# A transformer block on one core: when the expert weights are split, and in what order the tail runs

## The chip, the core and the metric

The program runs on one core of a Trainium2 chip. The metric is the device time of one execution in microseconds (us), from three runs of the kernel. The engines are TensorE (PE, matrix products; its clock is granted at 1.2 or 2.4 GHz), VectorE (DVE), ScalarE (ACT), GpSimd (POOL) and SyncE (SP), which issues the DMAs. Each engine runs its own list of instructions in order and waits on semaphores that the others count up.

## What is computed

```python
mod = (_silu(L0_c) @ L0_wmod).reshape(L0_c.shape[0], 6, 1, -1)
...
h = _layernorm(x, axis=-1) * (1 + ca) + sa
x = x + ga * _L0_attn_ref(h, L0_attn_Wqkv, L0_attn_bqkv, L0_attn_Wout, L0_attn_bout)
h = _layernorm(x, axis=-1) * (1 + cb) + sb
x = x + gb * _L0_ffn_ref(h, L0_ffn_router_w, L0_ffn_gate_up_proj, ...)
```

x has 4 batches of 512 tokens of width 256. The attention is causal, with 16 heads of 16. The FFN is a mixture: a shared expert that every token passes, and 8 routed experts (gate and up 256 x 1024, down 512 x 256 each), of which each token takes the one with the largest router logit, scaled by its sigmoid. All is float32.

## The kernel before

**Float32 products from f16 halves.** A matrix is scaled by 64 and split in a high f16 half and a low one, the rest; `split_mm` (L1392) forms three products of halves for one float32 product. The weights of the 9 FFN experts (index 8 is the shared one) come as 27 *units* of 1024 columns, 512 KB of float32 each: two for gate and up, one for down per expert. A unit is loaded by SP into one of the slots of `stage`; ScalarE writes its high half to its place in the large tile W (`split_high`, L885); then VectorE (`split_low`, L1153) or GpSimd (L714 scales the staged unit in place, L715 subtracts) writes the low half. The slot is then free for the next load.

**The loops.** Batch by batch (b = -1 to 3), 44 steps each. At step n TensorE computes transposed scores of batch b (`scores_t`, L1490) and plain scores of batch b+1 (`scores`, L1462 and L1464), VectorE takes the maxima of the latter (L1060), ScalarE the exponentials of the former (L838), GpSimd masks them (L693), and TensorE multiplies with the values (L1506). b = -1 has only the plain scores of batch 0, b = 3 only the transposed ones. TensorE has two banks for transposed scores, three in batch 3, so it may be two steps ahead of ScalarE. Side jobs hang on numbered steps (the tables SIDE and LAST): layer norms, the projections of q, k and v, the output projection, the second norm and the router of earlier batches; in batch 3 also the shared expert of batch 0. The halves of q and k and the maxima go through DRAM (`qk_d`, `ng_d`), and so do the rows of the modulation (`mod_d`, `gbb`): SP issues these transfers in one written order. The early tiles of the attention lie in W itself, so a weight unit can only be written to its place when what lies there is no longer needed:

```python
elif n == 6:
    ac.wait_ge(s_pv, 16 * (B - 1))
elif n == 9:
    ac.wait_ge(s_pv, 16 * B)
elif n == 18:
    ac.wait_ge(s_o, NT)
```

Nine units (0 to 8) are therefore split in the loops, three in batch 2 (steps 8, 19, 30) and six in batch 3 (two each at steps 5, 16, 27).

**The tail.** After the loops, parts 4 to 15 of the shared expert's gate and up run (`shared_up`, four 128-column parts per batch; each 12 matmuls of 512 columns), with ScalarE's `silu` (L895) and `hidden_high` (L902) and VectorE's `hidden` (L1168) and `hidden_low` (L1176). Between them stand the last batch's output projection, residual (L1103, L1105), second norm (L1110 to L1127), the transposes of h2 (L1547), router (`logits`, `route`), and the routing itself: `ranks`, `slots` (L1273 to L1282), the one-hots (L1283 to L1292), `inverse` and `places`, which give each of 23 row tiles its tokens. The 18 units 9 to 26 are split here, one or two behind each part. GpSimd gathers the first rows (L763).

**The routed stage.** 23 tiles of 128 gathered rows run through their expert's weights; it starts when all units are split. GpSimd adds the results to the output by indirect DMA (L781).

## Time and profile before

| | us |
|---|---|
| median of three runs | 500.05 (499.14 to 500.27) |
| the profiled execution | 499.79 |
| its span | 498.0 |
| TensorE busy | 405.4 (81%) |
| VectorE busy | 329.5 (66%) |
| ScalarE busy | 227.2 (46%) |
| GpSimd busy | 238.2 (48%) |

Busy time is what the hardware profiler recorded of instructions; a wait is the idle time of an engine ahead of an instruction, put down to what ended last before it. The first exponential starts at 72.02 us, the tail's first matmul at 280.12, the first routed matmul at 371.55.

### The profile page before, as it was taken

The page shows a single profiled execution, that of the slowest core. Times are in us where ns is not written, and L with a number is a line of the kernel's source. Part 1 is how long each engine was busy: PE and PEld are TensorE (multiplying, and loading weights), DVE is VectorE, ACT ScalarE, POOL GpSimd, SP SyncE. Part 2 cuts the span into 40 slices and gives each one's busy share as a digit, 9 for nine tenths or more (in the row PEclk, how much of TensorE's full clock was granted, in tenths as well). Part 3 has the DMA queues.
Part 4 walks back from the last instruction along what each step waited for, and adds up shares of the span by engine and source line. Part 5 has one row for each costly group of instructions (what it writes and reads, how often), then busy time and mean ns, then how long its engine had stood idle before and what let it go on. Part 6 is the DMA issues. An engine that isn't in the chain of part 4 may idle for free.

```text
span 498.0 us, 8328 instructions
## 1 busy us (share of the span) xinstructions
PE 405.4 (81%) x2898; PEld 229.9 (46%) x2898; DVE 329.5 (66%) x622; ACT 227.2 (46%) x403; POOL 238.2 (48%) x273
## 2 busy tenths in 40 slices
PE   3737789899989999889977964855928999999991
PEld 3214335445544455344443431622605666666661
DVE  3779799557968788986676399499383443443441
ACT  2612425776556666557764643273321233233230
POOL 1472843742368543754177368050860356556332
PEclk9978999999999999899999996796869999999998
DMA  7563256847201741132215063224661144443210
GB/s 252 168 161 75 64 111 145 246 134 187 40 0 47 173 78 40 42 120 68 60 47 170 1 205 90 86 84 138 176 194 43 33 80 78 86 78 75 44 21 1
DMA packets 39200, 49.08 MB, mean 99 GB/s; under 512 B 4788, under 2 KB 34100, under 8 KB 39160
## 3 DMA queue, kind: packets, MB, share of 16 engines
q1 hardware_dynamic: 34008, 40.41, 28.6%
q0 software_dynamic: 5152, 8.14, 8.3%
q8 instruction: 25, 0.41, 0.3%
q14 instruction: 15, 0.12, 0.1%
HBM read 33.70 MB, written 15.75 MB: 99 GB/s over the span
## 4 chain that ended last, share of the span: by engine, by line
PE 53%; DVE 19%; POOL 8%; issue 7%; ACT 6%; DMA 5%; SPq 1%; DVEq 0%; POOLq 0%; ACTq 0%
PE bank L1392 31%; PE bank L1506 5%; PE bank L1490 5%; PE bank L1462 4%; DVE W L1153 2%; DVE x_sb L1105 2%; PE bank L1721 2%; DVE mx L1060 2%; POOL W L674 2%; ACT W L813 2%; DVE W L1176 2%; PE bank L1464 2%; DMA qk_d<-W 1%; DVE rowg L1103 1%; DMA stage<-in_wmod 1%
## 5 line engine op out<-in xcount | busy, mean ns | idle before, releaser
L1392 PE MATMUL bank<-W 128*128 128x256 f16 (+2 forms) x756 | 110.0, 300 | 20.8 <-DVE W L1176 10.8
L838 ACT ACTIVATE W<-bank 128x512 f32<-128x512 f32 (+1 forms) x176 | 94.6, 562 | 66.4 <-PE bank L1490 64.6
L1060 DVE TENSOR_REDUCE mx<-bank 128x1 f32<-128x384 f32 (+3 forms) x176 | 104.4, 632 | 24.5 <-PE bank L1464 23.9
L1392 PEld LDWEIGHTS bank<-W 128*128 128x128 f16 x756 | 75.4, 102 | 56.2 <-DVE W L1176 12.0
L693 POOL TENSOR_SCALAR_AFFINE_SELECT W<-W 128x512 f32<-128x512 f32 x64 | 42.7, 670 | 73.8 <-ACT W L838 73.7
L1392 PE MATMUL bank<-W,h2T 128*128 x276 | 68.4, 385 | 10.0 <-DVE h2T L1350 9.2
L1462 PE MATMUL bank<-W 126*128 126x128 f16 (+3 forms) x256 | 64.9, 308 | 12.9 <-DMA W<-qk_d 7.9
L781 POOL DMA_INDIRECT out<-h2T,sidx x23 | 36.4, 1581 | 66.6 <-DVE h2T L1361 66.3
L1490 PE MATMUL bank<-W 128*128 128x512 f16 (+3 forms) x256 | 61.8, 303 | 2.6 <-ACT W L838 2.0
L1392 PE MATMUL bank<-h2T,W 128*128 128x512 f16 x192 | 48.1, 407 | 4.9 <-DVE W L1168 4.9
L1506 PE MATMUL bank<-W 128*32 128x128 f32 (+3 forms) x512 | 47.5, 444 | 4.4 <-POOL W L693 4.3
L1464 PE MATMUL bank<-maskb,identb 128*128 128x128 bf16 (+2 forms) x176 | 43.9, 250 | 0.0
L1392 PEld LDWEIGHTS bank<-W,h2T 128*128 128x128 f16 x276 | 26.7, 98 | 35.9 <-issue 15.4
L1354 DVE TENSOR_TENSOR W<-bank,W 128x512 f16<-128x512 f32 x23 | 15.9, 691 | 37.4 <-ACT W L966 37.4
L966 ACT ACTIVATE W<-bank 128x512 f16<-128x512 f32 x23 | 13.7, 597 | 55.1 <-PE bank L1721 55.1
L1462 PEld LDWEIGHTS bank<-W 126*128 126x128 f16 x256 | 23.6, 100 | 29.9 <-DVE mx L1060 13.0
L1490 PEld LDWEIGHTS bank<-W 128*128 128x128 f16 x256 | 21.4, 98 | 34.2 <-ACT W L838 17.7
L1392 PEld LDWEIGHTS bank<-h2T,W 128*128 128x128 f16 x192 | 19.4, 103 | 29.6 <-issue 6.6
L763 POOL DMA_INDIRECT rowg<-h_d,gidx x23 | 22.8, 991 | 19.0 <-DMA h_d<-rowg 12.5
L827 ACT ACTIVATE W<-bank,bqk 128x512 f16<-128x512 f32 (+1 forms) x32 | 20.3, 684 | 22.4 <-PE bank L1392 20.5
L885 ACT ACTIVATE W<-stage 128x1024 f16<-128x1024 f32 x24 | 24.7, 1055 | 8.4 <-DMA stage<-in_gup 8.3
L1153 DVE SCALAR_TENSOR_TENSOR W<-stage,W 128x1024 f16<-128x1024 f32 x18 | 25.5, 1431 | 3.7 <-ACT W L885 3.5
(166 smaller groups left out, 564.6 us busy)
## 6 DMA issues: line engine op xcount, KB each, us to landing
stage<-in_gup SPq DMA_DIRECT2D x14, 512.0 KB
qk_d<-W SPq DMA_DIRECT2D x48, 128.0 KB
W<-qk_d SPq DMA_DIRECT2D x32, 192.0 KB, 4.3
stage<-in_down SPq DMA_DIRECT2D x7, 512.0 KB
x_sb<-in_x SPq DMA_DIRECT2D x4, 512.0 KB, 9.0
h_d<-gbb SPq DMA_DIRECT2D x4, 512.0 KB, 4.6
h_d<-rowg SPq DMA_DIRECT2D x4, 512.0 KB, 5.7
out<-x_sb SPq DMA_DIRECT2D x4, 512.0 KB, 3.0
```

The source lines that it names most:

```text
L693: g.affine_select(out=d, in_=d, compare_op=ALU.is_ge, fill=0.0, base=0, pattern=[[0, 4], [1, P]], channel_multiplier=-1).then_inc(s_msk, 1)
L763: g.indirect_dma_start(rowg[:, r % RG, :], None, h2_d, bass.IndirectOffsetOnAxis(ap=gidx[:, r:r + 1].bitcast(U32), axis=0)).then_inc(s_gr[ ...
L781: g.indirect_dma_start(out.rearrange("b s n -> (b s) n"), bass.IndirectOffsetOnAxis(ap=sidx[:, r:r + 1].bitcast(U32), axis=0), ry[r % YR], ...
L838: a.activation(PT[j][:, i:i + m, :], t_bank(N)[:, 0:m * w].rearrange("p (i n) -> p i n", i=m), ACT.Exp).then_inc(s_exp, 1)
L885: a.activation(weights(n, 0), staged(n), ACT.Copy, scale=WS).then_inc(s_eh, 1)
L1060: v.tensor_reduce(mx_v[:, b % 2, hp0 // 4, par, i:i + m, t], SB[N % 3][:, 0:m * w].rearrange("p (i n) -> p i n", i=m), AX.X, ALU.max).then ...
L1153: v.scalar_tensor_tensor(weights(n, 1), staged(n), WS, weights(n, 0), ALU.mult, ALU.subtract).then_inc(s_el, 1)
L1392: i = t_.matmul(outp, l, r, start=(n == 0), stop=(n == len(prods) - 1), **kw)
L1462: t_.matmul(bk[:, w * i:w * (i + 1)], qs[r][0:P - 2, hp, par, P * t:w], ks[r][0:P - 2, hp, 0:w], start=(i == 0), stop=False, skip_group_ch ...
L1464: t_.matmul(bk[:, 0:m * w].rearrange("p (i n) -> p i n", i=m)[:, :, w - P:w], identb[:, :], maskb[:, :].unsqueeze(1).to_broadcast([P, m, P ...
L1490: q = t_.matmul(t_bank(N)[:, w * i:w * (i + 1)], ks[r][:, hp, P * j:P * (j + 1)], qs[r][:, hp, par, P * j:S], start=True, stop=True)
L1506: q = t_.matmul(OTb[32 * i:32 * i + 32, P * j:S], v1[b % 2][:, c:c + 32], PT[j][:, i], start=(j == 0), stop=(j == TT - 1), tile_position=( ...
```

## The change

All 27 units are now split in the loops; a table SPLITS gives each its step. They are counted by k, in the order in which they are split: the 18 units 9 to 26 come first (k = 0 to 17, "bounced"), the units 0 to 8 last (k = 18 to 26), the latter straight to their place in W as before. The halves of a bounced unit are written to one of two buffers `ob` in the tile rowg, stored to DRAM (`halves_out`, tensor w_d, 512 KB), and read into their place in W in the tail (`halves_in`), in three groups, as soon as the attention's tiles there are free. `split_high` of unit k waits until the store of k-2 has landed (s_bw). Of 11 bounced units (POOL_LOW) the low half is GpSimd's; ScalarE now also scales their staged unit in a second pass, and GpSimd only subtracts. There are three slots for loads; SP issues store k and then load k+3.

In the tail nothing is split. The last batch's second norm is two fused passes of VectorE (`centre2`, `modulate2`) where GpSimd did half of it; the engines' orders are written out; ScalarE itself issues the store of the last rows of h2; the one-hots are cut off from `slots`.

```diff
-SPLIT_AT = 5
 DEEP = 1
-POOL_UNITS = (9, 11, 13, 15, 17, 19, 21, 23, 25)
+DIRECT = 9
+BOUNCED = 3 * (E + 1) - DIRECT
+POOL_LOW = (0, 1, 2, 4, 6, 9, 10, 12, 14, 15, 17)
...
+SPLITS = {-1: {20: 0, 30: 1, 36: 2},
+          0: {2: 3, 7: 4, 12: 5, 17: 6, 21: 7},
+          1: {2: 8, 7: 9, 12: 10, 17: 11, 21: 12},
+          2: {2: 13, 7: 14, 12: 15, 17: 16, 21: 17, 28: 18, 33: 19, 38: 20},
+          3: {5: 21, 8: 22, 14: 23, 17: 24, 23: 25, 27: 26}}
...
+        w_d = nc.dram_tensor("w_d", [BOUNCED, P, 2, STEP], F16).ap()
...
+        ob = [rowg[:, 2 * k:2 * k + 2, :].rearrange("p r n -> p (r n)").bitcast(F16).rearrange("p (s n) -> p s n", s=2)
+              for k in range(2)]
...
+        def unit(k):
+
+            return k + DIRECT if k < BOUNCED else k - BOUNCED
+
+        def low_done(k):
+
+            by_pool = k in POOL_LOW
+            return (s_elp if by_pool else s_el, sum((m in POOL_LOW) == by_pool for m in range(k + 1)))
...
+        def split_part(k, part):
+
+            if k < BOUNCED:
+                return ob[k % 2][:, part].rearrange("p (s n) -> p s n", s=4)
+            return weights(unit(k), part)
...
-        def early_splits(b, gr):
-
-            if b == B - 2:
-                return range(gr, gr + 1) if gr < 3 else range(0)
-            if b == B - 1:
-                return range(3 + 2 * gr, 5 + 2 * gr) if gr < 3 else range(0)
-            return range(0)
-
-        def ffn_splits(n):
-
-            return (2, 2, 1, 2, 1, 1, 2, 2, 1, 2, 1, 1)[n - FC * DEEP]
...
+            def stage_load(k):
+                e, u = unit_list[unit(k)]
+                if k == 0:
                     sp.wait_ge(s_mp, 1)
-                before = [m for m in range(n) if slot(m) == slot(n)]
-                if before:
-                    sp.wait_ge(*split_done(before[-1]))
-                elif n >= 12:
-                    sp.wait_ge(s_u, FC)
-                dst, s = staged(n), s_eld[slot(n)]
+                if k >= 3:
+                    sp.wait_ge(*low_done(k - 3))
+                dst, s = staged(k), s_eld[k % 3]
...
+            def halves_out(k):
+                sp.wait_ge(*low_done(k))
+                sp.dma_start(w_d[k], ob[k % 2]).then_inc(s_bw[k % 2], 16)
+
+            def halves_in(k):
+                e, u = unit_list[unit(k)]
+                c = place(e)
+                dst = W[:, c:c + WX].rearrange("p (s n) -> p s n", s=2)[:, :, STEP * u:STEP * (u + 1)]
+                sp.dma_start(dst, w_d[k]).then_inc(s_wld, 16)
...
-            loaded = 0
+            for k in range(3):
+                stage_load(k)
...
-                while loaded < {-1: 0, 0: 3, 1: 3, 2: 6, 3: 12}[b]:
-                    expert_load(loaded)
-                    loaded += 1
+                if b == B - 1:
+                    for k in range(BOUNCED + 3, NU):
+                        stage_load(k)
+                elif b >= 0:
+                    for k in range(3 + 5 * b, 8 + 5 * b):
+                        halves_out(k)
+                        stage_load(k + 3)
...
+                    for k in range(3):
+                        halves_out(k)
+                        stage_load(k + 3)
...
-            for n in range(loaded, NU):
-                if n == 14:
-                    rows_out(B - 2)
-                if n == 23:
-                    rows_out(B - 1)
-                expert_load(n)
-
+            for k in range(2):
+                sp.wait_ge(s_bw[k], 8 * BOUNCED)
+            sp.wait_ge(s_pv, 16 * B)
+            for k in range(0, 9):
+                halves_in(k)
+            rows_out(B - 2)
+            sp.wait_ge(s_o, NT)
+            for k in range(9, 12):
+                halves_in(k)
+            sp.wait_ge(s_h2v, TT)
+            for k in range(12, BOUNCED):
+                halves_in(k)
...
-            def split_low(n):
-
-                po.wait_ge(s_eh, n + 1)
-                link(g.tensor_scalar(staged(n), staged(n), WS, 0.0, ALU.mult, ALU.add))
-                g.tensor_tensor(weights(n, 1), staged(n), weights(n, 0), ALU.subtract).then_inc(s_elp, 1)
+            def split_low(k):
+
+                if k not in POOL_LOW:
+                    return
+                po.wait_ge(s_es, sum(m in POOL_LOW for m in range(k + 1)))
+                g.tensor_tensor(split_part(k, 1), staged(k), split_part(k, 0), ALU.subtract).then_inc(s_elp, 1)
...
-            for n in (9, 11):
-                split_low(n)
             rstd(ve2, mv2, rs2, B - 1, s_mv2, s_rstd2)
-            for t in (2, 3):
-                modulate2(B - 1, t)
-            for n in (13, 15, 17, 19):
-                split_low(n)
             def gather(r):
...
+                ac.wait_ge(s_rows3, TT)
+                ac.dma_start(h2_d[S * b:S * (b + 1), 0:H].rearrange("(t p) n -> p t n", p=P), h2s).then_inc(s_h2w, 16)
...
+            def split_high(k):
+                ac.wait_ge(s_eld[k % 3], 32 * (k // 3 + 1))
+                n = unit(k)
+                if 2 <= k < BOUNCED:
+                    ac.wait_ge(s_bw[k % 2], 16 * (k // 2))
...
-                a.activation(weights(n, 0), staged(n), ACT.Copy, scale=WS).then_inc(s_eh, 1)
+                a.activation(split_part(k, 0), staged(k), ACT.Copy, scale=WS).then_inc(s_eh, 1)
+                if k in POOL_LOW:
+                    ac.wait_ge(s_eh, k + 1)
+                    a.activation(staged(k), staged(k), ACT.Copy, scale=WS).then_inc(s_es, 1)
...
+            def centre2(b):
+
+                ve.wait_ge(s_mv2, b + 1)
+                for t in range(TT):
+                    n = TT * b + t
+                    v.scalar_tensor_tensor(h2f[:, t], x_sb[:, n], mv2[:, n, 0:1], bc[:, b % 2, 2 * H:3 * H],
+                                           ALU.subtract, ALU.mult).then_inc(s_hm, 1)
...
+            def modulate2(b):
                 ve.wait_ge(s_hm, TT * (b + 1))
-                link(v.tensor_tensor(h2f[:, t], h2f[:, t], bc[:, b % 2, 2 * H:3 * H], ALU.mult))
-                v.tensor_tensor(h2f[:, t], h2f[:, t], bc[:, b % 2, H:2 * H], ALU.add).then_inc(s_h2v, 1)
+                ve.wait_ge(s_rstd2, b + 1)
+                for t in range(TT):
+                    n = TT * b + t
+                    v.scalar_tensor_tensor(h2f[:, t], h2f[:, t], rs2[:, n:n + 1], bc[:, b % 2, H:2 * H],
+                                           ALU.mult, ALU.add).then_inc(s_h2v, 1)
...
+            hidden(4)
+            attn_low(B - 1, 0)
+            attn_low(B - 1, 1)
+            hidden_low(4)
+            hidden(5)
+            residual(B - 1, 0)
+            residual(B - 1, 1)
+            stats2(B - 1)
+            hidden(6)
+            hidden_low(5)
+            centre2(B - 1)
+            hidden(7)
+            modulate2(B - 1)
+            hidden_low(6)
+            hidden_low(7)
+            hidden(8)
+            h2_low(B - 1, 0)
+            h2_low(B - 1, 1)
+            hidden(9)
+            logits(B - 1)
+            route()
+            shared_out(1, 0)
...
+            shared_up(4)
+            attn_turn(B - 1, 0)
+            attn_turn(B - 1, 1)
+            shared_up(5)
+            output(B - 1, 0)
+            output(B - 1, 1)
+            for n in range(6, 10):
                 shared_up(n)
-                if n == 4:
-                    attn_turn(B - 1, 0)
-                    attn_turn(B - 1, 1)
-                if n == 5:
-                    output(B - 1, 0)
-                    output(B - 1, 1)
-                if n == 8:
-                    shared_down(1, 0)
-                    h2_turn(B - 1, 0)
-                    h2_turn(B - 1, 1)
-                    shared_down(1, 1)
-                    router(B - 1)
-                if n == 9:
-                    ranks()
-                if n == 11:
-                    inverse()
-                if n == 12:
-                    shared_down(2, 0)
-                    shared_down(2, 1)
+            h2_turn(B - 1, 0)
+            h2_turn(B - 1, 1)
+            shared_down(1, 0)
+            router(B - 1)
+            shared_down(1, 1)
+            ranks()
+            for n in range(10, 13):
+                shared_up(n)
+            inverse()
+            shared_up(13)
+            shared_down(2, 0)
+            shared_down(2, 1)
+            shared_up(14)
+            rows_turn(0)
+            shared_up(15)
...
+            pe.wait_ge(*low_done(NU - 1))
+            pe.wait_ge(s_wld, 16 * BOUNCED)
```

**SP's order around batch 0.** From the stacks of batch 1 (W<-qk_d) on. Before:

```order
L479 DMA W<-qk_d 48x4x512 [waits s_qkw1_1]
L479 DMA W<-qk_d 48x4x512 x3
L565 DMA mod_d<-h2T 4x1024 [waits s_m4]
L485 DMA W<-mod_d 128x768 [waits s_md]
L568 DMA gbb<-mod_d 128x4x256
L489 DMA ng_d<-negm 32x2x128 [waits s_neg]
L496 DMA W<-ng_d 2x4x512 [waits s_ngw]
L496 DMA W<-ng_d 2x4x512
L540 DMA h_d<-gbb 128x4x256 [waits s_gbb]
L540 DMA h_d<-gbb 128x4x256 x3
```

Now, with w_d<-rowg the stores of halves and stage<-in_gup, in_down the loads:

```order
L481 DMA W<-qk_d 48x4x512 [waits s_qkw1_1]
L481 DMA W<-qk_d 48x4x512 x3
L520 DMA w_d<-rowg 128x2048 [waits s_elp]
L514 DMA stage<-in_gup 128x1024 [waits s_elp]
L520 DMA w_d<-rowg 128x2048 [waits s_elp]
L514 DMA stage<-in_gup 128x1024 [waits s_elp]
L520 DMA w_d<-rowg 128x2048 [waits s_elp]
L516 DMA stage<-in_down 128x4x256 [waits s_elp]
L579 DMA mod_d<-h2T 4x1024 [waits s_m4]
L487 DMA W<-mod_d 128x768 [waits s_md]
L582 DMA gbb<-mod_d 128x4x256
```

and on from there:

```order
L491 DMA ng_d<-negm 32x2x128 [waits s_neg]
L498 DMA W<-ng_d 2x4x512 [waits s_ngw]
L498 DMA W<-ng_d 2x4x512
L547 DMA h_d<-gbb 128x4x256 [waits s_gbb]
L547 DMA h_d<-gbb 128x4x256 x3
L520 DMA w_d<-rowg 128x2048 [waits s_el]
L514 DMA stage<-in_gup 128x1024 [waits s_el]
```

Three stores and three loads now stand ahead of mod_d, and the fourth store behind the four writes of gbb.

**ScalarE's order at the start of batch 0.** From the last q and k parts of batch 1 on, over the first exponentials (L838 before, L846 now). Before:

```order
L827 ACTIVATE W<-bank,bqk 128x512 [waits s_ql,s_qkw0_1,s_qkv]
L827 ACTIVATE W<-bank,bqk 128x512
L827 ACTIVATE W<-bank,bqk 128x512 [waits s_ql,s_qkv]
L827 ACTIVATE W<-bank,bqk 128x512
L838 ACT_TABLE_LOAD
L838 ACTIVATE W<-bank 128x512 [waits s_st] x4
L838 ACTIVATE W<-bank 128x384 [waits s_st] x4
L838 ACTIVATE W<-bank 128x512 [waits s_st] x3
L838 ACTIVATE W<-bank 128x512 [waits s_pv,s_st]
L838 ACTIVATE W<-bank 128x512 [waits s_st] x3
```

Now (L890 and L893 are the two passes of a split):

```order
L835 ACTIVATE W<-bank,bqk 128x512 [waits s_ql,s_qkv]
L835 ACTIVATE W<-bank,bqk 128x512
L890 ACTIVATE rowg<-stage 128x1024 [waits s_eld1]
L893 ACTIVATE stage<-stage 128x1024 [waits s_eh]
L890 ACTIVATE rowg<-stage 128x1024 [waits s_bw0,s_eld2]
L893 ACTIVATE stage<-stage 128x1024 [waits s_eh]
L846 ACT_TABLE_LOAD
L846 ACTIVATE W<-bank 128x512 [waits s_st] x3
L890 ACTIVATE rowg<-stage 128x1024 [waits s_bw1,s_eld0]
L846 ACTIVATE W<-bank 128x512 [waits s_st]
L846 ACTIVATE W<-bank 128x384 [waits s_st] x4
L890 ACTIVATE rowg<-stage 128x1024 [waits s_bw0,s_eld1]
```

and on from there, to step 14:

```order
L893 ACTIVATE stage<-stage 128x1024 [waits s_eh]
L846 ACTIVATE W<-bank 128x512 [waits s_st] x3
L846 ACTIVATE W<-bank 128x512 [waits s_pv,s_st]
L846 ACTIVATE W<-bank 128x512 [waits s_st]
L890 ACTIVATE rowg<-stage 128x1024 [waits s_bw1,s_eld2]
L846 ACTIVATE W<-bank 128x512 [waits s_st] x2
```

Units 1 and 2 (k) are split ahead of the first exponential, the second of them behind s_bw0, the landing of store 0; units 3, 4 and 5 stand between exponentials, unit 5 behind s_bw1, which then must count store 3.

**VectorE's order in the tail, from the statistics to the transposes of h2.** Before:

```order
L1113 BN_AGGR mv<-st 128x2 [waits s_dv]
L1113 BN_AGGR mv<-st 128x2 x3
L1153 SCALAR_TENSOR_TENSOR W<-stage,W 128x1024 [waits s_eh]
L1168 SCALAR_TENSOR_TENSOR W<-bank,W 128x512 [waits s_hh,s_hl,s_u,s_silu]
L1176 TENSOR_TENSOR W<-W 128x512 [waits s_hid,s_hh]
L1120 TENSOR_SCALAR rowg<-x_sb,mv,rs 128x256 [waits s_rstd2,s_mv2] x4
L1126 TENSOR_TENSOR rowg<-rowg,W 128x256 [waits s_hm]
L1127 TENSOR_TENSOR rowg<-rowg,W 128x256 [waits s_dv]
L1126 TENSOR_TENSOR rowg<-rowg,W 128x256 [waits s_hm]
L1127 TENSOR_TENSOR rowg<-rowg,W 128x256 [waits s_dv]
L1168 SCALAR_TENSOR_TENSOR W<-bank,W 128x512 [waits s_hh,s_hl,s_u,s_silu]
L1176 TENSOR_TENSOR W<-W 128x512 [waits s_hid,s_hh]
```

Now:

```order
L1123 BN_AGGR mv<-st 128x2 [waits s_dv]
L1123 BN_AGGR mv<-st 128x2 x3
L1188 SCALAR_TENSOR_TENSOR W<-bank,W 128x512 [waits s_hh,s_hl,s_u,s_silu]
L1196 TENSOR_TENSOR W<-W 128x512 [waits s_hid,s_hh]
L1138 SCALAR_TENSOR_TENSOR rowg<-x_sb,mv,W 128x256 [waits s_mv2]
L1138 SCALAR_TENSOR_TENSOR rowg<-x_sb,mv,W 128x256 x3
L1188 SCALAR_TENSOR_TENSOR W<-bank,W 128x512 [waits s_hh,s_hl,s_u,s_silu]
L1146 SCALAR_TENSOR_TENSOR rowg<-rowg,rs,W 128x256 [waits s_rstd2,s_hm]
L1146 SCALAR_TENSOR_TENSOR rowg<-rowg,rs,W 128x256 x3
L1196 TENSOR_TENSOR W<-W 128x512 [waits s_hid,s_hh] x2
L1188 SCALAR_TENSOR_TENSOR W<-bank,W 128x512 [waits s_hh,s_hl,s_u,s_silu]
L1151 TENSOR_TENSOR h2T<-bank,h2T 128x512 [waits s_hta] x2
```

The splits (L1153) are gone, the second norm is two passes of four operations for all tiles, and it is followed at once by the operations on which the transposes and the next parts wait.

## Rows read from the trace of the kernel before

**Rows 1.** The page: the span, and the chain that ended last by engine.
```profile
span 498.0 us, 8328 instructions
...
PE 53%; DVE 19%; POOL 8%; issue 7%; ACT 6%; DMA 5%; SPq 1%; DVEq 0%; POOLq 0%; ACTq 0%
```

**Rows 2.** Busy time by stage: stretch, length, engines, then PEclk, DMA share, GB/s.
```profile
122.00:178.00 56.00, 51.19 (x444) 28.40 (x443) 44.37 (x100) 34.70 (x66) 29.88 (x41) 1.00 0.32 74
178.00:229.00 51.00, 47.16 (x403) 25.04 (x402) 41.94 (x88) 30.48 (x57) 25.43 (x37) 0.97 0.21 58
...
280.00:371.50 91.50, 58.19 (x357) 32.83 (x355) 70.56 (x115) 38.53 (x55) 45.88 (x36) 0.80 0.43 130
371.50:498.00 126.50, 114.77 (x736) 74.94 (x736) 49.61 (x99) 33.62 (x68) 51.21 (x38) 0.97 0.29 55
```

**Rows 3.** Timeline of TensorE (PE) in the tail: start, duration, line, operation, idle before.
```profile
280.12 2.75 PE L1392 MATMUL bank<-h2T,W 128*128 128x512 f16 x12
...
298.77 5.15 PE L1392 MATMUL bank<-h2T,W 128*128 128x512 f16 x12 [4.63 <-DVE W L1168]
312.63 5.05 PE L1392 MATMUL bank<-W 128*128 128x256 f16 x24 [8.71 <-DVE W L1176]
...
318.39 2.78 PE L1392 MATMUL bank<-W 128*128 128x256 f16 x24
...
338.03 0.26 PE L1671 MATMUL bank<-ohv,rowg 128*128 128x23 f16 x4 [7.53 <-DVE rowg L1292]
...
359.60 2.75 PE L1392 MATMUL bank<-h2T,W 128*128 128x512 f16 x12
371.55 2.74 PE L1392 MATMUL bank<-W,h2T 128*128 x6 [9.20 <-DVE h2T L1350]
```

**Rows 4.** The lines of the splits: duration in ns, min/median/max, and where.
```profile
L885 ACT ACTIVATE W<-stage x24: 1039/1057/1069, 182.9 to 367.7; 128x1024 f16<-128x1024 f32 x24
...
L1153 DVE SCALAR_TENSOR_TENSOR W<-stage,W x18: 1192/1224/3135, 184.2 to 369.1; 128x1024 f16<-128x1024 f32 x18
...
L714 POOL TENSOR_SCALAR stage<-stage x6: 1045/1054/1479, 285.5 to 361.8; 128x1024 f32<-128x1024 f32 x6
...
L715 POOL TENSOR_TENSOR W<-stage,W x6: 2127/2162/2977, 286.6 to 363.0; 128x1024 f16<-128x1024 f32 x6
```

**Rows 5.** Timeline of VectorE (DVE) in the tail: residual, slots, one-hots.
```profile
293.49 0.41 DVE L1103 SCALAR_TENSOR_TENSOR rowg<-bank,W 128x256 f32<-128x256 f32 x1
...
328.12 0.28 DVE L1273 TENSOR_TENSOR cmpc<-bank,ij 128x128 f32<-128x128 f32 x1
...
337.20 2.49 DVE L1292 TENSOR_TENSOR rowg<-il,poslo 128x512 f16<-128x512 f32 x4
```

**Rows 6.** Timeline of SyncE's DMA issues (SPq) around batch 0.
```profile
76.54 1.77 SPq L479 DMA_DIRECT2D W<-qk_d  x4
78.36 0.34 SPq L565 DMA_DIRECT2D mod_d<-h2T  x1
83.42 0.34 SPq L485 DMA_DIRECT2D W<-mod_d  x1
...
84.28 0.50 SPq L489 DMA_DIRECT2D ng_d<-negm  x1
89.31 0.54 SPq L496 DMA_DIRECT2D W<-ng_d  x2
89.89 3.38 SPq L540 DMA_DIRECT2D h_d<-gbb  x4
```

**Rows 7.** DMA of 70 to 125 us: GB/s in 40 slices of 1.375 us.
```profile
GB/s 16 150 168 172 78 109 203 173 98 0 130 285 219 63 10 287 338 342 344 187 358 396 360 59 12 34 112 139 185 133 18 238 177 170 182 304 227 127 143 188
```

**Rows 8.** Timeline of ScalarE (ACT) around batch 0's start.
```profile
61.99 1.28 ACT L838 ACT_TABLE_LOAD   x1
72.02 2.84 ACT L838 ACTIVATE W<-bank 128x512 f32<-128x512 f32 x5 [8.75 <-PE bank L1490]
...
82.36 1.26 ACT L838 ACTIVATE W<-bank 128x512 f32<-128x512 f32 x2 [0.78 <-PE bank L1490]
```

175 lines of the change are left out of this document (63 added, 112 removed).

## The prediction

> **What bounds the kernel now.** First the page and the table by stage. The profiled execution took 499.79 us, of which its span is 498.0 [rows 1]; the median of the three runs is 500.05, so what I add to the profiled one stands 0.26 below the median, less than a measurement can tell (about 0.2%, 1 us either way, is what it can tell from no change). The chain that ended last is TensorE for 53% and VectorE for 19% [rows 1]. By stage [rows 2]: in the loops (two of the four batches are shown) TensorE is busy 51.2 of 56 and 47.2 of 51 us, so it has 4 to 5 us of slack per batch, VectorE 44.4 and 41.9, ScalarE 34.7 and 30.5. In the tail (280.0 to 371.5, batches 1 to 3 of the shared FFN and the routing) TensorE is busy only 58.2 of 91.5 us at a granted clock of 0.80. In the routed stage it is busy 114.8 of 126.5. The tail holds 33 us of idle TensorE: that is what can be won. The TensorE timeline [rows 3] says who held it: VectorE each time, 4.63 us at 298.77, 8.71 at 312.63, 7.53 at 338.03, 9.20 at 371.55. After such gaps the clock is at its lower level, 1.2 GHz: the twelve matmuls at 298.77 took 5.15 us where those at 280.12 took 2.75, the 24 at 312.63 took 5.05 where those at 318.39 took 2.78.
>
> **The tail: what is removed.** 18 units leave it. On ScalarE each was 1.06 us, on VectorE 9 at 1.22, on GpSimd 9 at 1.05 plus 2.16 [rows 4], all in the same orders as the work that TensorE waits for. Their loads go too, and with them SP's waits for a free stage.
> I build the new tail from TensorE's work. Busy 58.2 us, less the excess of the slow stretches (2.4 and 2.3 by the rows above, and two smaller ones of that kind: about 8 in all), gives 50 us at the upper clock, 2.4 GHz. To this I add the waits that the new order leaves:
> - Up to the transposes of h2 there is none: units 6 to 9 of the first projection (2.6 us each, start to start) cover the residual (0.8 us per tile, from 293.49 on [rows 5]), the statistics and the two fused passes of 4 x 0.42, which end some 18 us after the tail's start.
> - The ranks are issued at about 27.5 us. VectorE then needs a hidden_low that waits for ScalarE's row scaling, slots and one_hots (328.12 to 339.69, 11.6 us together [rows 5]) and three operations of 0.7; TensorE has three units, 7.8 us. It waits 2 us before unit 12 and 4.3 around the inverse, and runs one unit at the lower clock, 2.4 more.
> - At the end unit 15's hidden values, their halves and the first gathered rows: 2.7 us.
> 50 + 2 + 4.3 + 2.4 + 2.7 = 61.4 against 91.5: 30 us less, and the routed stage no longer starts at the lower clock (the six matmuls at 371.55 took 2.74 us, half of it excess [rows 3]), 1 more; I take **30.5 gained**, since each semaphore hop that I rounded away costs a little. Ends: 18 if half of the waits stay, 33 if all idle time goes.
> The read-back is 18 x 512 KB. Writes of that size moved at 287 to 344 GB/s [rows 7]: 9.4 MB in some 30 us, in three groups that start at about 0, 9 and 18 us of the tail, so it has landed by 33 us, and is wanted at 61. Cost nothing; its cover is 28 us. At half the rate it still fits, at a third it would cost some 30. The gathers wait for the last rows of h2, which ScalarE now sends itself and no longer stand behind SP's loads: nothing, the first gather is wanted 20 us later.
>
> **The loops: what is added.** Batch by batch, splits go from 0, 0, 0, 3, 6 to 3, 5, 5, 8, 6 (batch -1 first). Eleven of the 18 also get a second pass on ScalarE, and GpSimd keeps only the subtraction. By durations this is 29 passes of ScalarE, 31 us, seven splits of VectorE, 8.5 us, eleven of GpSimd, 24 us. Most of it has idle time to lie in. The waits are what matters. Each of two buffers must have been stored before the next but one unit is split, and the store is issued by SP in its own order.
> - **Wait A.** Split 2 stands at step 36 of batch -1, ahead of the first exponential in ScalarE's order, and wants store 0. SP issues store 0 only behind the last stacks of batch 1, at 78.36, where the small write of mod_d stands now [rows 6]. That small write had landed by 83.42, behind the same stacks; 512 KB at about 340 GB/s [rows 7] adds 1.5: 84.8. Split 2 and its second pass take 2.1, so the first exponential goes from 72.02 [rows 8] to 86.9, **14.9 us**. ScalarE had only a table load before it, so nothing hides this; TensorE runs two steps ahead and stops. Behind ScalarE stand GpSimd's masks and subtraction 2, and behind that SP's store 2.
> - **Wait B.** Split 5, at step 12 of batch 0, wants store 3. SP issues it behind store 2 (89.3, after subtraction 2 on GpSimd, 2.2), load 5, mod_d and its landing (5 us: 95), the three transfers of 84.28 with their landing (5 us more: 101) and the four writes of gbb to h2_d, 3.38 us to issue and about 7 until they have moved (at 89.89 now). That is 101.2 + 7.1 + 1.5 and the receipt, 1.4: store 3 has landed at 111.2. ScalarE ends exponential 12 at 83.62 now [rows 8]; with wait A, 1.0 for the lower clock less the two steps TensorE had ahead, and 1.5 for splits 3 and 4, at 101.0. So **10.2 us** more.
> - After B again 1.0, and splits 5, 6 and 7 together 2.5. Later stores are issued at least 3 us before they are wanted; I see no third wait.
> - Batches 1 and 2: 8.4 us more of ScalarE each, two more VectorE splits each (2.4), three subtractions on GpSimd each (6.6), one of them at step 21 just ahead of rstd and the low halves of q and k. Not shown before, so bounded: nothing if all of it fits the idle time, 17 if the whole of ScalarE's is on the path. VectorE at 82% is the nearest row [rows 2]: I take its 2.4, one subtraction of 2.2 and 0.4 for double passes, 5 us per batch, **10** together.
> - Batch 3: the same six splits, but one at a time and not two (2 x 1.06 on ScalarE in a row): 2.5 gained, after about 1.2 lost to the first load; **-2.5** as the net, between -6 and +2.
> Sum of the loops: 14.9 + 1.0 + 1.5 + 10.2 + 1.0 + 2.5 + 10 - 2.5 = 38.6. Whole: 38.6 - 30.5 = +8.1, and 499.8 + 8.1 = **508**.
>
> **Two rules weighed.** Store 0 is costed by the small write that landed 5.06 us after its issue [rows 6]. The Trainium skill, "DMA: Bandwidth & Descriptors", section "Anatomy of one DMA — SWDGE (gpsimd) path", fits a DMA from GpSimd's queue at about 2.0 us plus its bytes at 436 GB/s; an estimate from that page is 3.2 us for a store, landed at 81.6, and the whole would be 505. No run here shows such a store.
> When GpSimd's subtraction ran beside it, a VectorE split took up to 3.13 us and not 1.22 [rows 4], 1.9 more. The eight subtractions in batches 0 to 2 could each cost that, 15 us; I charge none beyond the 10 above, because the maxima read one operand, from PSUM. The Trainium skill, "SBUF — State Buffer", speaks of an exclusive shared port pair of VectorE and GpSimd, under which a VectorE operation with two SBUF inputs waits for the whole GpSimd one; by it the sum would go to 523 at most. The row agrees for that pair of operations.
>
> **Rivals.**
> 1. *Only wait A bites* (faster). If ScalarE reaches step 12 as store 3 lands (stores served out of turn, or the gbb writes moving faster than their 7 us), B's 10.2 and its 1.0 go: 508 - 11.2 = 497. For it: the engines moved 396 GB/s at best [rows 7]. Against: SP's order is fixed. The turning point: waits A and B together below 17 us. Chance 0.2 with all that ends below 499.
> 2. *The tail doesn't shrink so far* (slower). VectorE's chained small operations hold TensorE at every unit, or the read-back comes late; 18 won and not 30.5: 520. For it: the chain of slots and one_hots is untouched. Chance 0.13.
> 3. *The cost in the loops eats the gain exactly* (same): no more than 499 to 501, for instance B at 3 us. Chance 0.05.
> 4. *The loops don't take the splits*: more than one wait per batch, since SP is one queue; each costs as B, 10 us: 518. Chance 0.07, within the slower side.
>
> **How the numbers follow.** The forecast, both waits and a tail shorter by about 30, has 0.55, with its own range 502 to 515. Slower than by 0.2%: 0.55 + 0.13 + 0.07 = 0.75; same 0.05; faster 0.2. The range reaches from 494 (A alone, batches 1 and 2 at half price) to 521 (rival 2 with its round-off).
>
> **What would show it.** Right: in ScalarE's waits a DMA w_d<-rowg ahead of split 2 for about 20 us, the first exponential at 85 to 88; a second of 8 to 12 us at step 12; TensorE's idle there, with the lower clock behind each; the tail, from the first unit after the loops to the first routed matmul, in 60 to 64 us at a clock above 0.9; the routed stage unchanged. Wrong: the first exponential near 72, loops that end before 305, or a tail above 70 us.

## The result: 504.0 us against 500.0

| | before | after |
|---|---|---|
| median of five runs each, us | 500.05 (499.14 to 500.35) | 504.01 (503.34 to 504.91) |
| span of the profiled execution | 498.0 | 502.1 |
| first exponential | 72.02 | 87.82 |
| tail's first matmul | 280.12 | 320.40 |
| first routed matmul | 371.55 | 375.36 |

The ratio is 1.0086, with a 95% interval of 1.0067 to 1.0105: slower by some 4 us. Two changes of nearly 40 us stand behind that: the loops end 40.3 us later, the tail is 36.5 us shorter. The routed stage takes 126.7 us, before it took 126.5. (Of the four runs of `f2` below, one took 2173.7 us; it counts in no figure here.)

The page of the profile after, its span, busy time, chain by engine, and the two groups that are new:

```profile
span 502.1 us, 8371 instructions
...
PE 401.1 (80%) x2898; PEld 228.6 (46%) x2898; DVE 314.1 (63%) x620; ACT 236.3 (47%) x414; POOL 230.6 (46%) x262
...
HBM read 43.14 MB, written 25.18 MB: 136 GB/s over the span
...
PE 46%; DVE 14%; POOL 10%; DMA 10%; ACT 9%; issue 7%; SPq 3%; ACTq 0%; DVEq 0%; POOLq 0%
...
L890 ACT ACTIVATE rowg<-stage 128x1024 f16<-128x1024 f32 x18 | 19.0, 1058 | 28.6 <-DMA w_d<-rowg 28.6
...
w_d<-rowg SPq DMA_DIRECT2D x18, 512.0 KB, 3.0
```

DMA has doubled its share of the chain (5% before [rows 1]), and ScalarE's splits were held 28.6 us by the store of w_d alone. Busy time by stage (as in [rows 2]; a batch of the loops, then the tail, then the routed stage):

```profile
152.00:212.00 60.00, 51.26 (x441) 27.94 (x440) 48.43 (x101) 41.58 (x75) 36.79 (x44) 1.00 0.57 157
212.00:268.00 56.00, 47.23 (x398) 24.50 (x395) 46.42 (x91) 36.72 (x65) 32.48 (x40) 0.97 0.39 116
...
320.40:375.30 54.90, 48.67 (x356) 29.93 (x353) 41.79 (x106) 21.60 (x37) 11.49 (x14) 1.00 0.73 250
375.30:502.00 126.70, 114.86 (x736) 75.09 (x736) 49.65 (x99) 33.61 (x68) 51.11 (x38) 0.97 0.28 53
```

TensorE does the same work in batches 1 and 2 (51.3 and 47.2 us busy) and needs 60 and 56 us where it needed 56 and 51. In the tail its clock is 1.00 where it was 0.80, and its idle time has fallen from 33 to 6 us.

**Where the loops lost it.** Timeline of ScalarE (start, duration, line; L890 is the first pass of a split, L893 the second, L846 the exponentials):

```profile
84.36 1.06 ACT L890 ACTIVATE rowg<-stage 128x1024 f16<-128x1024 f32 x1 [20.26 <-DMA w_d<-rowg]
85.45 1.06 ACT L893 ACTIVATE stage<-stage 128x1024 f32<-128x1024 f32 x1
86.52 1.28 ACT L846 ACT_TABLE_LOAD   x1
87.82 1.08 ACT L846 ACTIVATE W<-bank 128x512 f32<-128x512 f32 x2
...
109.97 1.06 ACT L890 ACTIVATE rowg<-stage 128x1024 f16<-128x1024 f32 x1 [8.38 <-DMA w_d<-rowg]
```

and of SyncE's queue, where the stores (L520) stand behind stacks, mod_d and the writes of gbb (L547):

```profile
76.67 1.77 SPq L481 DMA_DIRECT2D W<-qk_d  x4
78.48 0.44 SPq L520 DMA_DIRECT2D w_d<-rowg  x1
...
99.83 3.40 SPq L547 DMA_DIRECT2D h_d<-gbb  x4
103.67 0.91 SPq L520 DMA_DIRECT2D w_d<-rowg  x1
```

Both waits are there, at the forecast places: 20.3 us of idle ScalarE ahead of split 2, which moves the first exponential by 15.8 us, and 8.4 us ahead of split 5. Behind each, TensorE's granted clock is at its lower level (0.50 from 88 to 90 us, and again from 110 to 115). `outs`, ScalarE's copy at the end of each quarter of a batch (L854), marks the positions; of its 16 rows, those at step 4 of batches 1 to 3 and the last one:

```profile
152.05 0.61 ACT L854 ACTIVATE W<-bank 128x512 f32<-128x512 f32 x1
...
211.99 0.61 ACT L854 ACTIVATE W<-bank 128x512 f32<-128x512 f32 x1
...
268.01 0.59 ACT L854 ACTIVATE W<-bank 128x512 f32<-128x512 f32 x1
...
319.26 0.60 ACT L854 ACTIVATE W<-bank 128x512 f32<-128x512 f32 x1 [1.25 <-PE bank L1533]
```

The same four stood at 122.64, 178.06, 229.43 and 278.98 before. So the loss is 29.4 us up to step 4 of batch 1, then 4.5, 4.65 and 1.7 in the three stretches that follow, which are called batches 1, 2 and 3 below.

**Where the tail won it.** TensorE's timeline has three gaps left:

```profile
355.75 0.26 PE L1697 MATMUL bank<-ohv,rowg 128*128 128x23 f16 x4 [0.34 <-DVE rowg L1313]
356.35 2.76 PE L1419 MATMUL bank<-h2T,W 128*128 128x512 f16 x12 [0.34 <-DVE W L1188]
...
375.36 2.74 PE L1419 MATMUL bank<-W,h2T 128*128 x6 [5.61 <-DVE h2T L1377]
```

### The profile page after: what moved, and what is told of

It reads as the page before. It is cut to its first block, busy times and chain, and to the rows that moved or that the text cites. A ratio compares the mean times of both kernels' runs of the same rounds, so it can differ in the third digit from the quotient of the medians.

```text
span 502.1 us, 8371 instructions
## 1 busy us (share of the span) xinstructions
PE 401.1 (80%) x2898; PEld 228.6 (46%) x2898; DVE 314.1 (63%) x620; ACT 236.3 (47%) x414; POOL 230.6 (46%) x262
## 4 chain that ended last, share of the span: by engine, by line
PE 46%; DVE 14%; POOL 10%; DMA 10%; ACT 9%; issue 7%; SPq 3%; ACTq 0%; DVEq 0%; POOLq 0%
PE bank L1419 32%; PE bank L1533 3%; PE bank L1517 2%; DVE mx L1070 2%; DMA w_d<-rowg 2%; DVE x_sb L1115 2%; DMA ng_d<-negm 2%; PE bank L1747 2%; DMA qk_d<-W 2%; ACT W L821 2%; ACT rowg L890 2%; PE bank L1489 2%; POOL W L693 2%; ACT W L846 2%; POOL W L712 2%
## 5 line engine op out<-in xcount | busy, mean ns | idle before, releaser
L846 ACT ACTIVATE W<-bank 128x512 f32<-128x512 f32 (+1 forms) x176 | 93.7, 563 | 51.5 <-PE bank L1517 50.4
L1419 PE MATMUL bank<-W 128*128 128x256 f16 (+2 forms) x756 | 106.1, 293 | 13.8 <-DVE x_sb L1115 5.3
L1419 PEld LDWEIGHTS bank<-W 128*128 128x128 f16 x756 | 73.4, 100 | 46.6 <-issue 13.0
L1517 PE MATMUL bank<-W 128*128 128x512 f16 (+3 forms) x256 | 63.1, 308 | 27.9 <-ACT W L846 27.3
L1489 PE MATMUL bank<-W 126*128 126x128 f16 (+3 forms) x256 | 66.0, 313 | 14.3 <-DMA W<-qk_d 8.2
L712 POOL TENSOR_SCALAR_AFFINE_SELECT W<-W 128x512 f32<-128x512 f32 x64 | 45.9, 722 | 67.0 <-ACT W L846 66.8
L1517 PEld LDWEIGHTS bank<-W 128*128 128x128 f16 x256 | 21.4, 99 | 61.5 <-ACT W L846 42.5
L1419 PE MATMUL bank<-h2T,W 128*128 128x512 f16 x192 | 43.3, 379 | 0.3 <-DVE W L1188 0.3
L735 POOL TENSOR_TENSOR rowg<-stage,rowg 128x1024 f16<-128x1024 f32 x11 | 23.4, 2124 | 24.2 <-ACT stage L893 24.0
L890 ACT ACTIVATE rowg<-stage 128x1024 f16<-128x1024 f32 x18 | 19.0, 1058 | 28.6 <-DMA w_d<-rowg 28.6
## 6 DMA issues: line engine op xcount, KB each, us to landing
qk_d<-W SPq DMA_DIRECT2D x48, 128.0 KB
```

Of the source, the lines that this page charges most:

```text
L712: g.affine_select(out=d, in_=d, compare_op=ALU.is_ge, fill=0.0, base=0, pattern=[[0, 4], [1, P]], channel_multiplier=-1).then_inc(s_msk, 1)
L735: g.tensor_tensor(split_part(k, 1), staged(k), split_part(k, 0), ALU.subtract).then_inc(s_elp, 1)
L846: a.activation(PT[j][:, i:i + m, :], t_bank(N)[:, 0:m * w].rearrange("p (i n) -> p i n", i=m), ACT.Exp).then_inc(s_exp, 1)
L890: a.activation(split_part(k, 0), staged(k), ACT.Copy, scale=WS).then_inc(s_eh, 1)
L1419: i = t_.matmul(outp, l, r, start=(n == 0), stop=(n == len(prods) - 1), **kw)
L1489: t_.matmul(bk[:, w * i:w * (i + 1)], qs[r][0:P - 2, hp, par, P * t:w], ks[r][0:P - 2, hp, 0:w], start=(i == 0), stop=False, skip_group_ch ...
```

## Experiments

Theory: SyncE's one queue, with store k and load k+3 behind unrelated transfers, makes waits A and B; the added work costs the 4.6 us in each of batches 1 and 2; the tail's gain is mostly the split work that left it. Rivals: a wait that is removed only turns up at the next store; the number of buffers is the cause, not the order; the tail's gain is the rewritten order; the read-back has little cover.

The experiments ran in three sets, each on a chip of its own; the kernel before was run in each, at 500.0, 500.1 and 499.7 us. All but one of them build on the change; "new order" is the kernel `e3`. One thing has to be known ahead of them. With the tail of the change, the time from the tail's first matmul to the first routed one goes by the set, whatever was edited:

| set | kernels | tail, us | gap ahead of the first routed matmul |
|---|---|---|---|
| (the result above) | the change | 55.0 | 5.6 |
| first | `e1`, `e2`, `e3` | 55.5 to 55.6 | 6.2 to 6.3 |
| second | `b3`, `b3` with the order, `f1` | 52.0 | 2.6 |
| third | `f2`, `f3`, `q1`, all together | 54.9 | 5.5 to 5.6 |

(The kernel without tail splits, of the first set, and `r1`, of the second, have other tails.) A difference of about 3 us between kernels of the second set and others is therefore not shown to come from the edit. Across sets the end of the loops (the last `outs`) is the better measure, though it too differs by 1.6 us between four traces with nearly the same loops (300.50 to 302.07 in `e3`, `r1`, `f3` and `q1`).

### One wait at a time

Store 0 and load 3 ahead of the first maxima's read-back (`e1`), or store 3 and load 6 ahead of the second's (`e2`):

```diff
                     maxima_out(b + 1, 0)
+                    if b < 0:
+                        halves_out(0)
+                        stage_load(3)
                     maxima(b + 1, 0)
...
-                    for k in range(3):
+                    for k in range(1, 3):
                         halves_out(k)
                         stage_load(k + 3)
```

`e2` does the same with `halves_out(3)` and `stage_load(6)`, between `maxima_out(b, 1)` and `maxima(b, 1)` at b = 0.

> Theory (the place of the stores in SyncE's program makes the waits): with store 0 and load 3 issued right behind the first maxima write (64.5 us) instead of behind the second half of the stacks (78.5), split 2 runs near 70 and the first exponentials come at 73 to 75 instead of 87.8. Store 1 is still issued near 79.5 and lands near 84, so split 3 at step 2 waits 7 to 9 us; wait B shrinks from 8.4 to 2 to 6, since SyncE no longer waits for split 2 before mod_d. Together 9 to 14 us off: 490 to 495 us. Rival 1 (the wait only moves to step 2 and to B, and the loop ends where it ended): 502 to 505 us. Rival 2 (wait A is a whole 15.8 us by itself, nothing behind it): 487 to 489 us.

> Theory: store 3 and load 6 issued between the write and the read-back of the second maxima of batch 0 (near 95 us instead of 103.7) land by 101, so ScalarE's 8.4 us at step 12 fall to under 2; wait A stays at 20.3. 6 to 9 us off: 495 to 498 us. Rival (the later batches had slack that took up wait B, or the maxima's read-back is delayed by as much): 502 to 505 us.

Measured: 500.5 us (1.0005 of before, 0.9984 to 1.0026; 3.5 under the change's 504.0) and 500.7 us (3.3 under). Both gains are far below the 9 to 14 and the 6 to 9 us that were expected, and both times fall between the ranges of theory and rival. ScalarE's splits with a wait, in the first:

```profile
70.99 1.06 ACT L893 ACTIVATE rowg<-stage 128x1024 f16<-128x1024 f32 x1 [6.27 <-DMA w_d<-rowg]
84.61 1.06 ACT L893 ACTIVATE rowg<-stage 128x1024 f16<-128x1024 f32 x1 [8.49 <-DMA w_d<-rowg]
105.50 1.06 ACT L893 ACTIVATE rowg<-stage 128x1024 f16<-128x1024 f32 x1 [7.52 <-DMA w_d<-rowg]
```

and in the second:

```profile
85.04 1.06 ACT L893 ACTIVATE rowg<-stage 128x1024 f16<-128x1024 f32 x1 [20.30 <-DMA w_d<-rowg]
112.49 1.06 ACT L893 ACTIVATE rowg<-stage 128x1024 f16<-128x1024 f32 x1 [3.08 <-DMA w_d<-rowg]
```

In the first, the 20.3 us became 6.3 at split 2 and 8.5 at split 3, which wants store 1, and split 5 still waits 7.5. In the second, the wait left split 5 (step 12), and 3.1 us came back at split 6 (step 17); by the `outs` at step 4 of batch 1 only 3.2 us of the 8.4 are gained. The rival, the wait moves on, holds for most of the price of either one alone.

### The whole order

Stores 0 to 5 with loads 3 to 8, each put where SyncE can issue it soonest: 0 behind the first maxima write, 1 behind its read-back, 2 behind `qk_out(1, 1)`, 3 while mod_d is on its way, 4 and 5 around the second maxima, all ahead of the writes of gbb (`e3`).

```diff
                     maxima(b + 1, 0)
+                if b < 0:
+                    halves_out(1)
+                    stage_load(4)
...
                     sp.dma_start(mod_d[:, :], m4[:, :]).then_inc(s_md, 16)
+                    halves_out(3)
+                    stage_load(6)
                     sp.wait_ge(s_md, 16)
```

> Theory: with stores 0 to 5 each issued as soon as SyncE can after its split, both waits fall to under 4 us together, the first exponentials come near 73 to 75, and the tail's first matmul near 298 instead of 320: 479 to 484 us, which is below both kernels. Rival 1 (the split work in the loops holds them, the waits hide part of it): only 10 to 15 us off, 489 to 494. Rival 2 (earlier stores and loads collide with the stacks and maxima, which come later): gain under 10 us.

Measured: 484.7 us, 0.9685 of before (0.965 to 0.972), 19.3 under the change. The theory's 479 to 484 is just missed, and its "under 4 us together" for the waits by more. The waits for w_d of 0.9 us and more, and the first exponential:

```profile
71.43 1.06 ACT L904 ACTIVATE rowg<-stage 128x1024 f16<-128x1024 f32 x1 [6.37 <-DMA w_d<-rowg]
...
74.89 1.68 ACT L860 ACTIVATE W<-bank 128x512 f32<-128x512 f32 x3
...
90.71 1.06 ACT L904 ACTIVATE rowg<-stage 128x1024 f16<-128x1024 f32 x1 [2.04 <-DMA w_d<-rowg]
98.02 1.06 ACT L904 ACTIVATE rowg<-stage 128x1024 f16<-128x1024 f32 x1 [0.92 <-DMA w_d<-rowg]
```

9.3 us where there were 28.6; the last `outs` is at 301.10, not 319.26. The first of them ends at 71.43, before the exponentials started in the kernel before (72.02), but the two passes and the table load behind it put the first exponential at 74.89. The two single moves gave 3.5 + 3.3; the whole order gives 19.3. Here the queue that serves two buffers had to be moved as a row.

### Buffers instead of order

A third buffer in the unused end of W, so that split k waits for store k-3 (`b3`; every `k % 2` of the buffers becomes `k % 3`), alone and with the new order:

```diff
+        ob.append(early(2 * STEP, F16).rearrange("p (s n) -> p s n", s=2))
...
-                sp.dma_start(w_d[k], ob[k % 2]).then_inc(s_bw[k % 2], 16)
+                sp.dma_start(w_d[k], ob[k % 3]).then_inc(s_bw[k % 3], 16)
```

> The change with a third buffer for the halves and SyncE's order as it was, so that split k waits for store k-3 instead of k-2. Theory (it is the order of SyncE's issues that sets the waits, since load k+3 stands behind store k): split 2 runs near 64 and the first exponentials come near 73, but split 3 at step 2 still waits until load 3 and store 0, issued at 78 to 79, have landed: 84 to 87, a wait of 8 to 12 us, and step 17 may wait for load 6 in place of wait B. 8 to 14 us off: 490 to 496. Rival (the missing buffer is the whole cause): both waits gone, 478 to 483, as in the kernel with the new order.

> Third buffer and the new SyncE order together. Theory: the three waits left in the new order (6.4, 2.0 and 0.9 us) go, unless a load takes their place: 477 to 482 us. Rival (the loads of stage land no earlier, so the waits only change their name): within 1.5 us of the 484.7 of the new order alone.

Measured: 494.2 us alone, 481.2 with the order, each in its theory's range. With the old order the name of the wait changes from the store to the load that stands behind it:

```profile
85.64 1.06 ACT L891 ACTIVATE rowg<-stage 128x1024 f16<-128x1024 f32 x1 [11.85 <-DMA stage<-in_gup]
110.01 1.06 ACT L891 ACTIVATE rowg<-stage 128x1024 f16<-128x1024 f32 x1 [4.36 <-DMA stage<-in_gup]
```

The second row is split 6, at step 17, as foreseen. But both times are of the set with the short tail. By the last `outs` (319.26 in the change) the buffer alone gains 4.8 us (314.50) and the order 18.2 (301.10): of the 9.8 us by the medians, about 3 are the tail. And behind the new order no gain of the third buffer shows in the loops: they end at 302.37, and the 3.5 us between 484.7 and 481.2 are the tail's (55.5 and 52.0). The three waits for w_d are gone, one of 2.2 us for a load has come, and what was won up to there (the third `outs` at 121.02, not 124.06) is lost at TensorE's next wait for the stacks, which SyncE issues at 123.22 here and at 122.47 with two buffers:

```profile
129.60 0.40 PE L1504 MATMUL bank<-W 126*128 126x128 f16 x4 [3.15 <-DMA W<-qk_d]
```

So the number fell in the theory's range by luck. Of the two, the order of SyncE's queue is the cause of most of the loss, and the number of buffers a small part.

### The work that was added to the loops

On the new order, all 18 low halves go to VectorE in one operation (`f1`: `POOL_LOW = ()`, which also removes ScalarE's second pass), or GpSimd scales its 11 units itself (`f2`):

```diff
-                po.wait_ge(s_es, sum(m in POOL_LOW for m in range(k + 1)))
+                po.wait_ge(s_eh, k + 1)
+                link(g.tensor_scalar(staged(k), staged(k), WS, 0.0, ALU.mult, ALU.add))
```

> The new SyncE order, and all 18 low halves on DVE in one operation (1.06 to 1.2 us each) instead of 11 of them on GpSimd behind ScalarE's second pass (1.06 us each). Theory (the 4.6 us that batches 1 and 2 each lost is ScalarE time ahead of the exponentials): 3 passes fewer in each batch, 2 to 3 us less in each, 6 to 9 us off in all: 476 to 479. Rival (DVE holds the loops as much): within 1.5 us of 484.7, or above.

> The new SyncE order, and GpSimd scales the 11 staged units itself (an operation of 1.05 us more for each) instead of ScalarE in a second pass. Theory (ScalarE's time in the loops is what counts): like the kernel with all low halves on DVE, 476 to 480 us, unless GpSimd's pair of operations slows DVE's small operations, then 480 to 484. Rival (GpSimd's masks come late behind the longer pair): 485 to 490.

Measured: 476.8 us (0.9532 of before, 0.9499 to 0.9565) for `f1`, and 484.7 (482.4 to 486.5) for `f2`, just above the second range of its theory and just below its rival's. By the positions of `outs`:

| | step 4 of batch 1 | batch 1 | batch 2 | batch 3 |
|---|---|---|---|---|
| before | 122.6 | 55.4 | 51.4 | 49.6 |
| the change | 152.1 | 59.9 | 56.0 | 51.3 |
| new order | 133.8 | 60.0 | 56.0 | 51.3 |
| and low halves on VectorE | 132.3 | 58.4 | 54.6 | 51.7 |
| or scaled by GpSimd | 136.1 | 58.5 | 54.0 | 52.3 |

Three second passes of ScalarE, 3.2 us, are worth 1.4 to 2.0 us of a batch wherever their work goes, less than the 2 to 3 expected. GpSimd's version gives it back before batch 1: its stores come later, and the waits for them are 12.4 us in all against 9.3. `f1` is 7.9 us faster than the new order by the medians, 10.6 by the two profiled spans; of these only 4.1 lie in the loops, 3.5 in the tail and 2.9 in the routed stage. The tail's part goes by the set, as said above, and the routed stage of that one trace of the new order is the longest of all (128.0 us; 125.1 in `f1`, 125.9 to 127.2 in the others). Within the second set `f1` is 4.4 us below `b3` with the order, so 4 to 5 us is what the edit is shown to give.

About 3 us of each batch's loss stay in `f1` (58.4 and 54.6 us, against 55.4 and 51.4). No run tells apart which of the first passes, VectorE's splits and the transfers holds them. In the trace of the change TensorE waits 3.6 us in batch 1 for the residual, VectorE's L1115, where it waited 0.6 before.

In batch 3 the six splits in near pairs, as before the change (`q1`, one line of SPLITS):

> The new SyncE order, and the six splits of batch 3 in near pairs (steps 5,6,16,17,27,28), as the kernel before had them, instead of steps 5,8,14,17,23,27. Batch 3 took 49.6 us before and 51.3 in the change, with one wait of 1.3 us for a load. Theory (the places of the splits and that wait make the 1.7 us): batch 3 falls to 49.6 to 50.3 us, 1 to 2 us off the 484.7. Rival (it is the units that come in from the batches before, not the places): 51 us or more.

Measured: 486.1 us; batch 3 took 51.8 us (249.25 to 301.02), and 51.2 to 52.7 in the traces of the new order with the places of the change. The rival: it isn't the places. A wait of 1.3 us for the load of unit 21 stayed, since SyncE issues it only behind batch 3's second maxima:

```profile
251.49 1.06 ACT L904 ACTIVATE W<-stage 128x1024 f16<-128x1024 f32 x1 [1.26 <-DMA stage<-in_gup]
```

### The tail: removed work or new order?

The kernel before without the tail's loads and splits, with its order of the tail otherwise kept (one of the cuts in its code):

```diff
-                for _ in range(ffn_splits(n)):
-                    split_high(split)
-                    split += 1
```

> The kernel before, without the loads 12 to 26 and without the 18 splits of the tail (it leaves out the weights of the six experts that they serve: every routed tile takes those of one loaded expert). Order of the tail otherwise as it was. Theory (the tail shrinks because the split work leaves it): tail 56 to 66 us of 91.4, and the DVE operations of slots and one-hots that took 0.8 to 2.0 us beside GpSimd's splits take about 0.2; whole 465 to 475 us. Rival (the rewritten order of the tail gives a good part of the 36.5 us): tail 70 to 80 us, whole 479 to 489.

Measured: 475.1 us. The table by stage, of that tail (280.49 to 347.13):

```profile
280.49:347.13 66.64, 53.68 (x356) 31.12 (x354) 43.26 (x106) 21.48 (x37) 14.20 (x18) 0.92 0.20 64
```

91.4 us becomes 66.6 without the splits, and 55.0 with the rewritten order of the tail as well: 24.8 us of the 36.5 are the removed work, 11.7 the rewritten tail. TensorE still idles 5.1 us for `hidden_low` and 2.5 for the one-hots there, and its clock falls behind them (24 matmuls took 4.46 us and 12 took 5.30, where others of their kind took 2.78 and 2.75). The theory holds for two thirds of the gain, just outside the range that it gave (56 to 66 us), and the rival for one third.

VectorE's chain of small operations, of the kernel before, with GpSimd's splits beside it:

```profile
328.76 0.82 DVE L1276 TENSOR_TENSOR_SCAN ends<-onesE,ntile 128x8 f32<-128x8 f32 x1
329.61 0.17 DVE L1277 TENSOR_TENSOR base<-ends,ntile 128x8 f32<-128x8 f32 x1
329.81 1.98 DVE L1278 TENSOR_SCALAR base<-base 128x8 f32<-128x8 f32 x1
...
334.16 1.98 DVE L1286 TENSOR_TENSOR poslo<-posr,poshi 128x16 f32<-128x16 f32 x1
```

```profile
328.51 1.05 POOL L714 TENSOR_SCALAR stage<-stage 128x1024 f32<-128x1024 f32 x1 [18.22 <-ACT W L885]
329.64 2.13 POOL L715 TENSOR_TENSOR W<-stage,W 128x1024 f16<-128x1024 f32 x1
...
333.97 2.13 POOL L715 TENSOR_TENSOR W<-h2T,W 128x1024 f16<-128x1024 f32 x1
```

and the same operations of the change, where GpSimd is idle:

```profile
348.53 0.17 DVE L1295 TENSOR_TENSOR_SCAN ends<-onesE,ntile 128x8 f32<-128x8 f32 x1
...
348.94 0.17 DVE L1297 TENSOR_SCALAR base<-base 128x8 f32<-128x8 f32 x1
...
351.95 0.18 DVE L1307 TENSOR_TENSOR poslo<-posr,poshi 128x16 f32<-128x16 f32 x1
```

Each long one began while a GpSimd operation ran and ended with it (331.79 and 331.77; 336.14 and 336.10); L1277, which began in the gap of 0.08 us between two of them, took 0.17. The Trainium skill, "SBUF — State Buffer", section "SBUF: two separate sides", states an exclusive lock held for the whole instruction; the traces agree. In the kernel without the splits the same operations take 0.17 to 0.18 as well. With L1284 (0.90 us, 0.18 in the change) the four long ones are 5.0 us longer, which is the whole difference between the 11.6 us of `slots` and one-hots before and the 6.6 of both other kernels.

### The read-back

> The new SyncE order, and each read-back transfer issued three times (the two extra ones go into the idle staging tiles; output unchanged). In the change the 18 read-backs landed some 32 us into the tail and were wanted at 55. Theory (hidden, with 23 us of cover): 36 more at some 400 GB/s are 47 us more, less the cover: 22 to 28 us above the 484.7. Rival (the cover is smaller because gathers and rows share the queue, or the transfers slow other work): over 32 us above; rival 2 (reading costs little more): under 15.

Measured: 515.6 us, 30.9 above, between the theory's 28 and the first rival's 32. In the kernel with the new order alone the traffic (last column, GB/s) ends some 2 us behind 330 (349 GB/s from 331 to 332, 67 from 332 to 333):

```profile
325.00:330.00 5.00, 5.00 (x82) 4.16 (x79) 3.97 (x13) 3.43 (x7) 0.00 (x0) 1.00 1.00 367
330.00:335.00 5.00, 5.00 (x25) 2.25 (x23) 4.55 (x16) 2.62 (x5) 0.00 (x0) 1.00 0.45 164
335.00:340.00 5.00, 4.32 (x34) 2.23 (x33) 5.00 (x12) 1.53 (x3) 0.00 (x0) 1.00 0.02 5
```

Its first routed matmul is at 357.78: 26 us of cover. With three times the reads that matmul is released at 387.67, so the last transfer that it needs ended some 56 us later; less the cover, 30. In the change itself the traffic falls off shortly behind 350 (385 GB/s up to there, 121 from 350 to 351), 30 us into the tail, so the read-back is hidden there too, with a cover of about 25 us where 28 were forecast. One thing was not expected: the rows of batch 2 stand behind nine read-backs in SyncE's queue, and ScalarE, which must wait for them, stood 18.1 us there, TensorE 17.2. In the change that place costs nothing only because the nine go out in 8 us.

### The last gap, and all together

> The new SyncE order, and TensorE transposes the first gathered rows behind the last shared unit instead of ahead of it. The idle time ahead of the first routed matmul is 5.6 to 6.3 us in four traces and 2.6 in four others. Theory (the first gather lands late in some of them, and the transposes hold the last shared unit behind them): the gap is 2.6 to 4 us here, 0 to 3 us off the 484.7. Rival (it is something else, or the rows now come too late): gap 5.5 us or more, 484 to 487.

> New SyncE order, third buffer, all low halves on DVE, and the first gathered rows transposed behind the last shared unit. If the four gains add (19.3, 3.5, 7.9 and 0 to 3 us from 504.0): 470 to 474 us. Rival (the third buffer and the DVE halves take the same time away): 474 to 477.

`f3` (`rows_turn(0)` behind `shared_up(15)`): 486.1 us, gap 5.6, as the 5.5 of the three others of its set. Not the place of the transposes. All together: 481.1 us (five runs, 480.9 to 482.8), above both ranges and above the 476.8 of `f1`, though its loops end 0.9 us earlier (last `outs` at 296.05 and 296.97). The sum that was expected had counted the second set's shorter tail, 3.5 us, as a gain twice. Against the 486.1 of `f3` and `q1`, in its own set, it is 5.0 us faster. Its tail has the long gap and `f1`'s the short one; the first routed matmuls of `f1`, then of all together:

```profile
350.10 1.47 PE L1433 MATMUL bank<-W,h2T 128*128 x6 [2.64 <-DVE h2T L1391]
```

```profile
352.08 2.74 PE L1434 MATMUL bank<-W,h2T 128*128 x6 [5.53 <-DVE h2T L1392]
```

The gap was 2.6 us in four traces (`b3`, `b3` with the order, `f1`, and the kernel without tail splits) and 5.5 to 6.3 in eight. Where it is long, `silu` and `hidden` of the last two shared units wait some 3 us each for TensorE, though its records show no pause. TensorE's records are the same on both sides: its last shared unit starts 46.60 us into the tail in `b3`, `e3`, `q1` and the change. With the tail of the change the gap was the same in all kernels of one set and different between the sets; the kernel without tail splits, with the older order of the tail, had 2.6 in the first set. What decides it stays open, and so does whether it is the chip: no kernel with this tail was run in two sets.

## Why the prediction came out as it did

Forecast 508, measured 504.0, in the range and on the forecast side. The two waits, the longer loops and the shorter tail are all there, at their places. That the total is off by 4 only is partly luck: the tail came out 6.0 us shorter than forecast, and the loops 1.7 and the routed stage 0.3 longer, against it. Three smaller steps failed: the sign of batch 3, the 1 us counted for the routed stage, and what was to hold batches 1 and 2.

| term | forecast | measured |
|---|---|---|
| wait A (first exponential) | 14.9 | 15.8 |
| wait B | 10.2 | 8.4 |
| the loops up to batch 1, with both | 31.1 | 29.4 |
| batches 1 and 2 | +10 | +9.2 |
| batch 3 | -2.5 | +1.7 |
| loops | +38.6 | +40.3 |
| tail (the forecast with 1 us of the routed stage) | -30.5 | -36.5 |
| routed stage | in the tail's | +0.3 |

- **Wait A.** Store 0 landed at 84.36 (forecast 84.8). What was missed is the 1.28 us table load, which stood ahead of the wait in the kernel before [rows 8] and stands behind split 2 now: "ScalarE had only a table load before it" is the sentence that should have charged it.
- **Wait B** came at step 12 of batch 0 and was 8.4 us: ScalarE was there at 101.6 (forecast 101.0), and store 3 had landed by 109.97 (111.2). From the start of the gbb writes to the landing it took 10.1 us, as summed (7.1 + 1.5 + 1.4), though no row gave the 1.4 of the receipt. What was put 1.4 us too late is that start, 101.2 and not 99.83: store 2 was issued at 88.73 (89.3), and mod_d had landed by 93.80 (95).
- **Batches 1 and 2.** The size held, the parts didn't. Moving eleven more low halves to VectorE made the loops shorter, which speaks against the 2.4 us for its splits, and the second passes of ScalarE, put at 0.4, are 1.4 to 2.0 us of each batch. The other 3 us of each are not explained by a run.
- **Batch 3** is a step that failed. The 2.5 us forecast as gained were 1.7 lost, within the bounds of -6 to +2: one split at a time instead of two gained nothing, and near pairs gave no other length. A wait of 1.3 us for the load of unit 21 stands in that batch, where no split of the kernel before waited; no run took it away, so its part in the 1.7 isn't shown.
- **The tail** is where the error lies: 54.96 us, outside the 60 to 64 named as the sign of being right. "slots and one_hots (11.6 us together)" took 6.6 us now (347.89 to 350.08 and 351.33 to 355.69). The durations of the rows before held waits for GpSimd's splits, which the change takes away; with that, the 2 and 4.3 us of TensorE's waits and the slow unit went to 0.7. The end, costed at 2.7 us, was 5.6 instead. TensorE's work, put at 50 us at the upper clock, is 48.7; with 6 of idle time it makes the 55. The bound of 33 us, "all idle time goes", left out what the clock gives back: the 91.5 us less the prediction's own 50 are 41.5, and the 36.5 lie below that. The "1 more" of the routed stage was not gained: its first six matmuls took 2.74 us again, behind the 5.6 us of idle time.
- **The stores.** The 18 took 3.0 us to land in the median, store 0, behind the stacks, 5.9. The estimate of 3.2 us from the Trainium skill, "DMA: Bandwidth & Descriptors", section "Anatomy of one DMA — SWDGE (gpsimd) path", fits the undisturbed store, though these come from SyncE's queue; at the place that decided, behind the stacks, it was 5.9. The total of 505 by that estimate is nearer to 504.0 than the forecast, but by luck: it has store 0 landed at 81.6, and that was 84.36.
- **The shared port.** Charged nothing in the loops, and the seven VectorE splits of the 18 took 1.23 us in the median, 1.52 at most: right there. The same lock was overlooked in the tail, where it was a gain.
- **Rivals.** Only wait A bites: no; removing either wait alone moved it on. The tail doesn't shrink so far: no. The loops eat the gain exactly (499 to 501): no, 504.0. More than one wait per batch: not in the change, but it is what each half of a repair met.

## What to carry to other kernels

When work moves under a loop, place its transfers first: a store that frees one of two buffers belongs in its queue right where its data are ready, and the whole row of stores has to be moved, since a single repair hands the wait to the next one (3.5 and 3.3 us, against 19.3). With the order repaired and the second pass gone the change is worth having: 476.8 us against 500.1 in one set, and 481.1 against 499.7 with the third buffer in another. Before gains of single edits are added up, see in which stage of the trace each one lies: 3 us in a stage that the edit doesn't touch are not its gain. And durations read beside a busy GpSimd aren't VectorE's own: before costing a chain of small operations, look at what GpSimd runs in the same microseconds.

## What was not expected of the hardware

- VectorE operations on 8 or 16 columns took 0.82 to 1.98 us beside a GpSimd operation, among them one with a single input tile (L1278, TENSOR_SCALAR), and 0.17 to 0.18 alone.
- Where the gap was 5.5 us or more, TensorE's first six routed matmuls took 2.74 us, the lower of its levels; where it was 2.6 us they took either 1.47 (`f1`) or 2.71 to 2.74 (`b3` alone and with the order, and the kernel without tail splits). One gap, both levels.
- The same tail took 52.0 us in one set of runs and 54.9 or 55.5 in two others, the same to 0.1 us inside each, though TensorE's last shared unit starts at 46.60 us in traces of all of them.
